# Layer 0's expert stage: the second bias is added by VectorE while it empties PSUM, in place of one small matrix product per tile

## The reference, cut to what matters

```
x = x + _L0_xattn_ref(_layernorm(x), ctx_1024, ctx_1024, mask_1x1xSxS2_ik0, ...)
x = x + _L0_ffn_ref(_layernorm(x), ...)
...
def _L0_ffn_ref(hidden_states, w_red, wg, W1, b1, W2, b2):
    ...
    h = gelu(x @ W1[idx] + b1[idx])      # 256 -> 512, idx is the row's expert
    o = h @ W2[idx] + b2[idx]            # 512 -> 256, b2 is [8, 256]
    o = o * scores[:, None]
```

## Time and profile before

| | |
|---|---|
| median time of three runs | 596.76 us |
| span of the profiled execution | 601.6 us |
| PE busy | 554.9 us (92%) |
| DVE busy | 259.3 us (43%) |
| ACT busy | 208.8 us (35%) |
| mean granted TensorE clock | 0.943 of full speed |
| layer 0's expert stage | about 159.5 to 240.5 us of the span |
| tiles in it | 16 |

### The profile page before, as it was taken

The page is one execution under the profiler, slowest core; times in us unless marked ns, Lnnn a source line. Parts: engine busy times, 40 slices in busy tenths (PEclk is TensorE's granted clock), DMA queues, the critical chain, the costliest instruction groups (busy, mean ns, idle before and its releaser), DMA issues.

```text
span 601.6 us, 8029 instructions
## 1 busy us (share of the span) xinstructions
PE 554.9 (92%) x2865; PEld 362.5 (60%) x2867; DVE 259.3 (43%) x766; ACT 208.8 (35%) x393; POOL 84.6 (14%) x124
## 2 busy tenths in 40 slices
PE   2998999889889999798699989999999999999995
PEld 1456455554678888665344444665667676767663
DVE  5375777552247463473646543252222221222120
ACT  1444444442446552235533463321112112211221
POOL 2300600022102100200000000007212112211222
PEclk9997999996999999659879898999999999999998
DMA  8400006992112220393000006202672112211211
GB/s 304 139 1 0 1 2 220 367 354 104 36 35 89 73 86 27 128 369 124 2 0 1 2 0 218 71 1 99 199 254 34 32 26 36 32 31 27 36 17 25
DMA packets 38783, 54.17 MB, mean 90 GB/s; under 512 B 3341, under 2 KB 32461, under 8 KB 38736
## 3 DMA queue, kind: packets, MB, share of 16 engines
q1 hardware_dynamic: 29552, 40.07, 19.9%
q0 software_dynamic: 4336, 6.75, 5.7%
q10 hardware_dynamic: 4848, 6.76, 3.4%
HBM read 39.05 MB, written 14.51 MB: 89 GB/s over the span
## 4 chain that ended last, share of the span: by engine, by line
PE 85%; DVE 7%; ACT 4%; DMA 2%; issue 2%; POOL 0%; SPq 0%; DVEq 0%; POOLq 0%; ACTq 0%
PE PS L1670 16%; PE PS L714 10%; PE PS L725 9%; PE PS L1695 8%; PE PS L742 6%; PE PS L1594 5%; PE PS L1471 4%; PE PS L1482 4%; PE PS L300 4%; PE PS L320 4%; PE PS L1605 3%; PE PS L1683 2%; PE PS L289 2%; PE PS L732 2%; DVE W L878 2%
## 5 line engine op out<-in xcount | busy, mean ns | idle before, releaser
L878 DVE TENSOR_REDUCE W<-PS 128x2 f32<-128x512 f32 x128 | 84.9, 686 | 70.2 <-PE PS L714 69.5
L714 PE MATMUL PS<-W 32*128 32x256 f32 x512 | 100.1, 442 | 7.2 <-ACT W L576 5.3
L725 PE MATMUL PS<-W 32*128 32x512 f32 x256 | 98.3, 706 | 1.7 <-ACT W L970 1.3
L1670 PE MATMUL PS<-W,PR 128*128 x304 | 97.9, 466 | 0.0
L714 PEld LDWEIGHTS PS<-W 32*128 32x128 f32 x512 | 65.7, 207 | 41.0 <-issue 20.4
L1670 PEld LDWEIGHTS PS<-W,PR 128*128 128x128 f32 x304 | 54.9, 190 | 30.2 <-issue 6.0
L1695 PE MATMUL PS<-W,PR 128*128 x228 | 56.1, 388 | 0.7 <-DVE PR L1716 0.7
L1695 PEld LDWEIGHTS PS<-W,PR 128*128 128x128 f32 x228 | 41.7, 189 | 15.0 <-issue 7.3
L2398 POOL DMA_INDIRECT out<-PR,slots x19 | 29.5, 1555 | 144.3 <-ACT PR L2343 117.4
L970 ACT ACTIVATE PR<-PS 128x512 f32<-128x512 f32 x64 | 35.2, 597 | 22.8 <-PE PS L725 22.6
L970 ACT ACTIVATE W<-PS 128x512 f32<-128x512 f32 x64 | 34.9, 598 | 23.1 <-PE PS L725 23.1
(11 more groups left out here) (262 smaller groups left out, 694.4 us busy)
## 6 DMA issues: line engine op xcount, KB each, us to landing
W<-in_L_ffn_W SPq DMA_DIRECT2D x16, 512.0 KB, 9.9
W<-in_rguT SPq DMA_DIRECT2D x5, 1408.0 KB, 10.3
W<-in_rdT SPq DMA_DIRECT2D x5, 640.0 KB, 11.4
W<-in_mask SPq DMA_DIRECT2D x3, 1024.0 KB, 14.0
scratch_rows<-W SPq DMA_DIRECT2D x1, 2860.0 KB, 14.7
W<-in_rguT ACTq DMA_DIRECT2D x2, 1408.0 KB, 11.0
VR<-scratch_rows SPq DMA_DIRECT2D x19, 130.0 KB, 2.0
scratch_x<-W SPq DMA_DIRECT2D x1, 2048.0 KB, 14.2
```

Source lines behind the costliest of these rows:

```text
L714: m = pe.matmul(PS[:, u % 3, q * FK:(q + 1) * FK], QT[r:r + 32, g, c:c + 128], KT[r:r + 32, g, b * FK:(b + 1) * FK], start=True, stop=True)
L725: pe.matmul(PS[:, 3 + u % 3, :], KT[r:r + 32, g, b * FK + kb * 128:b * FK + (kb + 1) * 128], QT[r:r + 32, g, 512 * b:512 * (b + 1)], start ...
L878: dve.tensor_reduce(NM[:, s % 2, q:q + 2, c], PS[:, u % 3, :].rearrange("p (q n) -> p q n", q=2), AX, ALU.max).then_inc(sem("m_free"), 1)
L1670: m = pe.matmul(PS[:, b0 + hf, 0:352], XS[:, r % 2, k, :], W[:, bass.ds(slot * SLOT + o, 352)], start=(k == 0), stop=(k == 1))
```

## The change

The ninth product of each tile goes. ACT no longer takes results out of PSUM; DVE does, with an addition of the expert's bias row, which lies spread over all 128 partitions in `B2`: two arrays of four experts each, 4 KB a partition, 1 MB in all. `B2` lies where the attention of layer 0 keeps weights until its last outputs are made, so SP waits for these (bank 6, use `("outputs", 0, 7)`), issues the two transfers, and goes on to the loads of the tiles behind them. On DVE, `take_y(i - 1)` stands behind `beside(i)`. The preparation of the three bf16 parts at the start goes as well. The diff, cut to its core:

```diff
-    bsf = W[0:8, a0 + 14336:a0 + 14592]
-    bsp = W[0:8, a0 + 14592:a0 + 14976].bitcast(BF16).rearrange("p (s n) -> p s n", s=3)
-    BS = W[0:3, 16384:17408].bitcast(BF16)
+    B2 = [W[:, o:o + 1024].rearrange("p (e n) -> p e n", n=D) for o in (a0 + 6144, a0 + 9216)]
...
-        pool.wait_ge(sem("small"), 16)
-        pool.tensor_copy(bsp[:, 0, :], bsf).then_inc(sem("bias_parts"), 1)
...
-        pool.dma_start(bd.rearrange("s e n -> e s n"), bsp).then_inc(sem("bd"), 16)
-        pool.wait_ge(sem("bd"), 16)
-        pool.dma_start(BS, bd.rearrange("s e n -> s (e n)")).then_inc(sem("bs"), 16)
...
-        act.dma_start(bsf, A["L0_ffn_b2"]).then_inc(sem("small"), 16)
...
-                pe.matmul(PS[:, bk, 0:D], HT0[:, i % 2, j, :], W[:, o:o + D], start=(j == 0), stop=False)
-            o = (i % E0) * D
-            pe.matmul(PS[:, bk, 0:D], onesb[0:3, :], BS[:, o:o + D], start=False, stop=True).then_inc(sem("down"), 1)
+                m = pe.matmul(PS[:, bk, 0:D], HT0[:, i % 2, j, :], W[:, o:o + D], start=(j == 0), stop=(j == NJ0 - 1))
+            m.then_inc(sem("down"), 1)
...
     def ffn0_act(tiles, beside):
-        def take_y(i):
-            act.wait_ge(sem("down"), i + 1)
-            if i > 1:
-                act.wait_ge(sem(f"stored{i % 2}"), 16 * (i // 2))
-            act.activation(YO0[:, i % 2, :], PS[:, 3 + i % 2, 0:D], ACT.Copy).then_inc(sem("y_out"), 1)
...
-            if i > first:
-                take_y(i - 1)
             beside(i)
-        take_y(last)
+
+    def load_b2():
+
+        for h in range(2):
+            rows = A["L0_ffn_b2"][4 * h:4 * h + 4, :].rearrange("(a e) n -> a e n", a=1)
+            sp.dma_start(B2[h], rows.to_broadcast([128, 4, D])).then_inc(sem("b2"), 16)
 
     def ffn0_dve(tiles, beside):
+        def take_y(i):
+            e = i % E0
+            dve.wait_ge(sem("down"), i + 1)
+            if i > 1:
+                dve.wait_ge(sem(f"stored{i % 2}"), 16 * (i // 2))
+            dve.tensor_tensor(YO0[:, i % 2, :], PS[:, 3 + i % 2, 0:D], B2[e // 4][:, e % 4, :], ALU.add).then_inc(sem("y_out"), 1)
...
-        take_x(tiles[0])
+        first, last = tiles[0], tiles[-1]
+        take_x(first)
+        dve.wait_ge(sem("b2"), 32)
         for i in tiles:
-            if i < tiles[-1]:
+            if i < last:
                 take_x(i + 1)
             beside(i)
+            if i > first:
+                take_y(i - 1)
+        take_y(last)
...
         sp.dma_start(xk, X[:, 0:4, :]).then_inc(sem("kept"), 16)
+        sp.wait_ge(*full(6, ("outputs", 0, 7)))
+        load_b2()
         ffn0_sp(MAIN, {0: (sem("scattered"), SCATTERED[0]), E0: (sem("scattered"), SCATTERED[1])})
```

More of the change, by code:

```diff
@@ L182, in build @@
     PS = ctx.enter_context(nc.psum_tensor("PS", [128, 8, 512], F32))
-    bd = nc.dram_tensor("scratch_bias", [3, 8, D], BF16).ap()
     xs = nc.dram_tensor("scratch_x", [4 * TILES0 * 128, D], F32).ap()
@@ L1498, in ffn0_act @@
     def ffn0_act(tiles, beside):
-        def take_y(i):
-            act.wait_ge(sem("down"), i + 1)
-            if i > 1:
-                act.wait_ge(sem(f"stored{i % 2}"), 16 * (i // 2))
-            act.activation(YO0[:, i % 2, :], PS[:, 3 + i % 2, 0:D], ACT.Copy).then_inc(sem("y_out"), 1)
-        first, last = tiles[0], tiles[-1]
         for i in tiles:
@@ L1786, in fast_pe @@
         pe.wait_ge(sem("nv_raw"), 2)
-        pe.wait_ge(sem("bs"), 16)
         pe.wait_ge(sem("b1"), 1)
@@ L2201, in general_dve @@
         dve.wait_ge(sem("e_free"), 32)
-        dve.wait_ge(sem("bs"), 16)
         dve.wait_ge(sem("x_bo"), NT)
```

## The result

The changed kernel takes 602.70 us (median of 20 runs, 598.45 to 609.47) where the kernel before takes 596.65 (20 runs, 594.53 to 603.63): ratio 1.0081, 95% interval 1.0054 to 1.0108. Slower, clear of the prediction's own mark of 0.5%, and outside the predicted range (594.3 to 601.2) on the high side. The profiled execution took 598.95 us with a span of 597.7, so time is span plus 1.25; it is one of the quicker ones. Its span is shorter than that of the profile before (601.6), which had lost more to a low granted clock ahead of the stage.

The account below looks back on a forecast made before the run. The prediction took PE to bound the stage, loads and DVE close behind. Saved products of 3.15 us were eaten by waits (+0.3); with the entrance (+0.75) that is +1.05 on 596.76, giving 597.8 us, range 594.3 to 601.2.

Parts of the forecast that it names:

- the prediction's own mark of 0.5%: Whole kernel: about 0.5% (3 us) is what a measurement tells from no change; slower means over 599.7 us.
- The sum inside the stage: Tile 0 to first queries: 3.15 us of removed products all eaten by later waits, +0.3 us at the stage's end.
- the tail: After the last product: DVE takes tile 15, then normalizes queries until 242.1, where ACT ended at 241.80.
- tile 14's: PE before tile 14: load issued late behind iteration 11's DVE block, PE idles 1.8 us, 0.5 behind before.
- tile 9's: PE before tile 9: load lands at 200.0 where PE wanted it at 199.5; PE 0.27 us ahead.
- the last `down`: Last tile: `down(15)` waits for DVE's `take_y(13)` until 238.8, PE ready at 238.2; its end moves from 240.47 to 240.7.
- The work at the very start ... goes at no gain: Kernel start: removing one 8 KB load, five POOL instructions and two small transfers gains nothing, being off the chain.
- The entrance: Before tile 0: SP issues 1 MB of bias ahead of the tiles' loads, +0.75 us, bounds 0 and +2.9.
- The estimate that made the entrance free: Before tile 0: 2.0 us per transfer plus bytes at 436 GB/s lands 1.18 MB after 4.7 us, costing nothing.
- The slow bias: Rival at the entrance: bias moves at 201 GB/s, costing 2.9 us, time 600.0 us; chance 0.13.
- The rival of the clock: Rival: new PE idle, decided before tile 14 from about 2 us on, drops the clock; 3 us lost, 600.8; chance 0.14.
- +1.05: Whole kernel: the stage's +0.3 us together with the entrance's delay.

Follow-up runs that it names:

- Both halves: Two edits of the kernel before: product of three partitions left out, without layer 0's second bias (592.75 us, 0.9930); DVE copying results from PSUM, products kept (604.64 us, 1.0068).
- the one with the fill later: Changed kernel with GpSimd's fill of 128 x 2048 zeros moved behind VectorE's first masks: 602.59 us, ratio 1.0104.
- the filler: Kernel before with the bias transfers ahead of the first loads, plus eight 128 x 128 products on PE ahead of tile 0: 602.03 us, ratio 1.0012.
- the bias load alone: Kernel before plus the bias transfers ahead of the first tiles' loads and DVE's wait for them; products and ACT's exits stay: 601.78 us, ratio 1.0061.
- the three edits in the stage: Changed kernel, bias behind first loads, results taken inside or before statistics, first queries normalized before tile 15's take: 600.04 us (0.9989); on another chip 593.09 us (0.9895).

## Why the prediction was wrong

- **The sum inside the stage was right, in part by luck.** "All 3.15 us eaten by later loads, one bank and the tail", +0.3: the accounts show no change within 0.3 us (83.2 to 83.7 before, 83.4 to 83.7 after). Both halves were tried alone, 2.9 less and 2.8 more. The waits stand where it put them: tile 14's 2.40 us for 1.8, tile 9's 0.42 for about 0.5, the last `down` 0.76 for 0.6, the tail 0.2 longer. But two sizes were off and cancelled: at tile 12 PE stood 1.2 to 1.6 us ahead of the profile before (less the fall at tile 2), where the sum had 0.9, and from tile 12 to tile 14 it lost 1.8 to 2.1, where the sum had 1.4.
- **The step that failed: "The work at the very start ... goes at no gain".** Gain was asked about, loss was not. The removed work carried a wait on POOL, and what was queued behind that wait moved 20 us forward, beside VectorE's operations on the chain that starts the kernel. In the traces it cost 1.1 to 1.5 us, for which the sum had nothing. The diff showed the move before any run: the fill stands directly behind the lines that go.
- **The entrance** was mis-sized within its bounds: 1.16 to 1.43 us of idle time in the profiles of the changed kernel, and 1.0 to 1.6 in the accounts, for +0.75. Bias and first tile landed at 154.20, 5.9 us after the first issue at 148.26, where the earlier trace rows gave 5.2 and 0.3. That row was misread: its 228 GB/s are what two queues moved together, SP's 0.73 MB and ACT's 0.45 MB, not SP's queue alone. The estimate that made the entrance free (4.7 us) was wrong too. The Trainium skill, page "DMA: Bandwidth & Descriptors", section "Anatomy of one DMA", gives its price for transfers that GpSimd issues; these were issued by SP. The slow bias, +2.9, was not seen either.
- **The rival of the clock** had the right sign and the wrong place. It looked to tile 14, "from an idle of about 2 us on": tile 14 waited 2.26 to 2.56 us and the clock held in all three profiles of the changed kernel, though it fell behind the same 2.40 us (from 225 on) in the one with the fill later. Nor is 1.76 us safe, as the prediction read from one execution: in another of the kernel before the clock fell behind it. What fell was the clock around tile 2, behind idle times of 1.16, 0.68 and 1.96 us. In the six profiles with a wait at the entrance a fall came there each time; in thirteen without one (the filler not counted) a fall came around tile 2 five times. That the wait brings the fall is likely by these counts and not shown by an experiment: the filler left it open. One such fall cost 1.7 us, not 3.
- **What the terms add up to.** Entrance and start give 2.9 us, and with them in place of +1.05 the forecast would have been 599.7; with one fall of the clock on top, 601.4. Measured are 4.7 us between the medians of 601.22 and 596.55. Two timings agree: the bias load alone gave 1.0061, and 1.3 us for the fill, 0.2%, would make that 1.0083, where the changed kernel gave 1.0081. One speaks against it: with the fill moved back the ratio was 1.0104 and not 1.006. What lies between 2.9 and 4.7, and the 6 us between the medians of all runs, are executions at a lower mean clock: 12 of the changed kernel's 20 were at 0.952 or less, with a median of 0.9505; the kernel before had medians of 0.952 to 0.954 on the four chips for which its clock is recorded. At equal clock there is one run each to compare: at 0.951 the changed kernel took 601.2 and at 0.954 599.7, the kernel before 598.4 to 599.0 and 596.4 to 596.8 on two chips, but 601.8 and 600.4 on a third, so this says little. The extra fall at the entrance is one part of the lower clock (1.7 us). Longer falls also stand at 50 to 60 in two of three profiles of the changed kernel and one of three of the kernel before, and at 132 to 148 in two of three of both. Whether the change makes them more frequent stays open, and so does why moving the fill mended the start and not the time.

## What to carry to other kernels

A removed instruction takes its waits with it: look at what stood behind them, on each engine, even far from the change. An exit moved to a busier engine costs by its place and not by its length: put inside the long blocks of DVE, ahead of the tail's norms, and with the bias behind the first loads, the same change becomes 1% faster than the kernel before on one chip (0.9895, and 0.9908 with the fill late), 0.8% by the ratio and 0.4% by the medians on another (fill late), and equal to it on a third (0.9989, fill early). With a clock that falls by execution, compare sections less their low-clock loss; the medians alone would have hidden that the stage came out as computed.

## What was not expected of the hardware

- A VectorE `tensor_scalar` on 128 x 4 numbers took 1.62 us beside a 1.80 us fill on GpSimd, and ended 0.03 us behind it; with two fills of 0.94 us it stood for one only. Two operations with two inputs passed beside the same fill in 0.15 to 0.17 us.
- A wait of 2.40 us on PE before tile 14 left the granted clock at 1.00 in the changed kernel and was followed by a fall to 0.50 in the one with the fill later; waits of 1.16, 0.68 and 1.96 us close together came with a fall, and waits of 0.68 and 1.75 us did in one execution of the kernel before and not in two others.
- What falls cost came in steps of about 1.7 us: ahead of tile 0 the 20 profiles lost 1.7, 5.1, 6.8 or 10.3. Over the span the three profiles of the kernel before lost 24.7, 26.5 and 34.5 us.
- The interval of one chip doesn't hold for the next: the same kernel with the three edits in the stage gave 0.9989 (0.9950 to 1.0028) on one and 0.9895 (0.9857 to 0.9932) on another. At a mean clock of 0.951 the kernel before took 598.4 to 599.0 us on three chips and 601.8 on a fourth.
